# A gated-linear-attention and mixture-of-experts layer on eight cores: each sequence divided 18 tiles and 14 instead of 16 and 16, with the code of the two halves chosen by a flag

## The chip, the cores and the metric

The kernel runs on all 8 cores of one Trainium2 chip, four sequences of 4096 tokens, two cores for each sequence. The cores exchange nothing. The metric is device time in microseconds (us) of the slowest core. Before the change it is 1550.89 us, the median of 3 runs (1548.65 to 1551.49).

## The reference

Each token is a row of 1024 numbers. With `xn = layernorm(x)` the layer returns `x + attention(xn) + ffn(xn)`. Cut to what matters:

```
q, k, v = xn@Wq, xn@Wk, xn@Wv            # 4 heads: 256, 256 and 512 wide
g  = logsigmoid(xn@Wgk1@Wgk2 + b) / 16   # a decay for each channel of the key
S_t = exp(g_t) * S_{t-1} + k_t^T v_t     # state 256 x 512 for each head, along the sequence
o_t = q_t @ S_t * 256**-0.5
attention = (rmsnorm(o) * rms_w * silu(xn@Wg)) @ Wo
ffn = xn + sum over the 2 best of 4 experts of w_e * LN(relu(LN(xn@W1_e+b1))@W2_e+b2)
```

The state S runs through the whole sequence, so the core with the later tokens needs the state that the earlier tokens leave.

## The kernel before

**Work and stages.** A tile is 128 tokens. Every core owns 16 tiles (`T = 2048`), in four blocks of four, and runs one and the same program.

1. *Prefix* (`p_LN`, `p_T`, `p_gk`, `p_scan`, `p_Eop`, `p_K`, `p_KT`, `p_M`): the state that the first 2048 tokens of the sequence leave. For each block of four tiles the rows are normalized (ScalarE, `p_xtm`), transposed on TensorE (`p_xT`), the decays go through exp and ln on ScalarE and a running sum on VectorE (`p_L`), and the keys are multiplied by them (`p_kd`) and transposed by DMA (`p_kdT`). `p_M` sums x^T k over all 16 tiles (256 matmuls), and 64 more matmuls with Wv give the state `s_W`. All eight cores do this; on the cores with the first half the result is multiplied by 0 (L718, `cvals[:, 3]`).
2. *Attention*: four blocks. A block has 16 groups of silu gates (`groupG`, 8 matmuls each), and then four units, one for each head (`unit`): queries and keys (`groupQ`, `groupK`), values (`groupV`), the next head's decays (`gates`), and woven between them (`merge`) the recurrence of the unit before (`gla_A`, `gla_C`, four steps). `gla_end` scales the four output rows-blocks of a unit by their rms (L963, VectorE), transposes them by DMA and stores them to the DRAM tensor `og_d`. The next block's tokens are loaded, normalized and transposed as side work of units 0 and 1, the router (`m_route`) in unit 2. In the last block unit 1 carries `lists`, which sorts the tokens by expert: 32 indirect DMAs write the lists to DRAM, one after another on GpSimd (L1129).
3. *Output projection* (`wo_head`, `wo_half`): for each tile 34 matmuls, with `s_ogl` loaded back from `og_d` (`load_ogl`, 2 MB a block) and the token rows `s_xr`. In the same stretch GpSimd issues the expert weights (`load_e`): float32 in DRAM, cast to bfloat16 by the DMA on its way to SBUF, 16 pieces an expert.
4. *Experts*: 35 slots (`NSLOT`) of 128 token rows each. A slot's rows are gathered by indirect DMA, transposed by DMA (`s_xgT`), and go through `f_z1` (16 matmuls, VectorE adds b1 and takes statistics), a norm (`s_zh`), `f_th` (8 transposes on TensorE, 8 relus on ScalarE), `f_z2` (16 matmuls, VectorE adds b2 and takes statistics), a norm (`s_z`), a multiplication (`s_y`) and an indirect DMA that adds the rows to the output. The stages of neighbouring slots are interleaved in one hand-written loop.

**What sets the order.** Every engine runs its own list in program order, and a helper `P.emit` puts the semaphore waits in front. SyncE's queue carries all transposing DMAs, the `s_ogl` loads and the stores of the output; GpSimd's queue carries the weights, the loads of x in the attention stage, the stores to `xn_d` and `og_d`, the list writes, and gathers; ScalarE's queue the `s_xr` loads. Within a queue a DMA whose wait isn't over holds all behind it. The addresses of an expert's weights come from registers that TensorE and VectorE load at each slot (L89), and six slots have one conditional wait on TensorE (`wait_if`).

Line 334 is every plain matmul (`mm`), 339 every transpose on TensorE, 343 every plain DMA of GpSimd, 348 and 350 SyncE's; so the rows are told apart by their tiles.

## Time and profile before

| | |
|---|---|
| Median of 3 runs | 1550.89 us |
| The profiled execution | 1549.63 us, with a span of 1548.1 us from the first to the last instruction of its slowest core (core 1) |
| Spans of the 8 cores | 1542.5, 1548.1, 1509.7, 1528.1, 1511.6, 1513.7, 1515.4, 1513.2 us |
| Busy, core 1 | TensorE 1088.4 us (70%), VectorE 679.7 (44%), ScalarE 570.8 (37%), GpSimd 213.4 (14%) |
| Chain that ended last | TensorE 43%, issue 15%, VectorE 14%, ScalarE 11%, DMA 9% |

On core 1 the prefix lasts to 327 us, the attention blocks to 926, the output projection to 1151, and the experts to the end. PE is TensorE, PEld its weight loads, DVE VectorE, ACT ScalarE, POOL GpSimd, SP SyncE; "q" behind one of these is its instruction queue. The time behind `<-` in square brackets is what ended the idle time ahead of an instruction, inferred from semaphores.

### The profile page before, as it was taken

The page shows a single profiled execution, that of the slowest core. Times are in us where ns is not written, and L with a number is a line of the kernel's source. Part 1 is how long each engine was busy: PE and PEld are TensorE (multiplying, and loading weights), DVE is VectorE, ACT ScalarE, POOL GpSimd, SP SyncE. Part 2 cuts the span into 40 slices and gives each one's busy share as a digit, 9 for nine tenths or more (in the row PEclk, how much of TensorE's full clock was granted, in tenths as well). Part 3 has the DMA queues.
Part 4 walks back from the last instruction along what each step waited for, and adds up shares of the span by engine and source line. Part 5 has one row for each costly group of instructions (what it writes and reads, how often), then busy time and mean ns, then how long its engine had stood idle before and what let it go on. Part 6 is the DMA issues. An engine that isn't in the chain of part 4 may idle for free.

```text
span 1548.1 us, 21016 instructions; the slowest of 8 cores (1509.7 to 1548.1 us)
## 1 busy us (share of the span) xinstructions
PE 1088.4 (70%) x4906; PEld 461.4 (30%) x4906; DVE 679.7 (44%) x1340; ACT 570.8 (37%) x1095; POOL 213.4 (14%) x266
## 2 busy tenths in 40 slices
PE   2347484998798589858888453966487777777772
PEld 1123131433333233323333121422133333333331
DVE  2353342012573266326635443410015666776664
ACT  3633411043434334434444111210104656565653
POOL 3000010000000000000001532050012222222211
PEclk9977586877999799979999766987688999999996
DMA  9931058501221422144119127999739756556643
GB/s 202 157 82 28 0 82 163 82 28 38 60 67 28 116 49 55 28 116 69 35 28 151 22 50 198 221 224 196 214 84 158 133 104 109 95 104 108 105 73 57
DMA packets 171934, 151.66 MB, mean 98 GB/s; under 512 B 127500, under 2 KB 139820, under 8 KB 171792
## 3 DMA queue, kind: packets, MB, share of 16 engines
q0 software_dynamic: 41168, 86.61, 30.4%
q1 hardware_dynamic: 128352, 55.33, 17.4%
q10 hardware_dynamic: 2304, 8.39, 1.7%
q8 instruction: 53, 0.87, 0.3%
q14 instruction: 57, 0.47, 0.1%
HBM read 117.84 MB, written 40.21 MB: 102 GB/s over the span
## 4 chain that ended last, share of the span: by engine, by line
PE 43%; issue 15%; DVE 14%; ACT 11%; DMA 9%; another core or an unknown queue 2%; DVEq 2%; SPq 2%; ACTq 0%; POOL 0%; POOLq 0%
PE pb L334 39%; DMA s_ogl<-og_d 4%; PE pb L1319 3%; ACT s_hT L1387 2%; DVE s_bnf L1334 2%; DVE p_L L509 2%; ACT s_zh L1372 2%; SPq L348 1%; PE pb L339 1%; DVE s_L L822 1%; DVE s_bn L407 1%; DMA s_xgT<-s_xg 1%; DVE s_bn L408 1%; DVE s_z L1324 1%
## 5 line engine op out<-in xcount | busy, mean ns | idle before, releaser
L334 PE MATMUL pb<-s_wo,s_ogl 128*128 128x512 bf16 x512 | 123.4, 397 | 77.4 <-DMA s_ogl<-og_d 77.1
L1319 PE MATMUL pb<-s_we,s_xgT 128*128 x560 | 132.4, 392 | 29.3 <-DMA s_xgT<-s_xg 13.5
L334 PE MATMUL pb<-s_wv,s_xnT 128*128 128x512 bf16 x512 | 131.1, 405 | 14.2 <-ACT s_v L890 6.3
L334 PE MATMUL pb<-s_wg,s_xnT 128*128 128x512 bf16 x512 | 129.0, 415 | 14.4 <-ACT s_silu L841 13.9
L938 DVE SCALAR_TENSOR_TENSOR s_W<-s_W,s_eb,pb 128x512 bf16<-128x512 bf16 x128 | 89.8, 742 | 96.1 <-PE pb L334 62.3
L1319 PE MATMUL pb<-s_we,s_hT 128*128 x560 | 128.6, 384 | 0.0
L1387 ACT ACTIVATE s_hT<-pb,s_gbs 128x128 bf16<-128x128 bf16 x280 | 103.9, 450 | 10.7 <-PE pb L339 9.7
L1324 DVE TENSOR_TENSOR s_z<-pb,s_b 128x512 bf16<-128x512 f32 x140 | 90.4, 685 | 27.4 <-PE pb L1319 21.1
L1185 DVE TENSOR_TENSOR s_xr<-s_xr,pb 128x512 f32<-128x512 f32 x32 | 22.0, 688 | 172.3 <-PE pb L334 172.3
L944 ACT ACTIVATE s_sq<-pb 128x512 bf16<-128x512 f32 x64 | 38.2, 596 | 158.9 <-PE pb L334 109.8
L1418 POOL DMA_INDIRECT out<-s_y,s_list x35 | 55.2, 1577 | 276.1 <-DVE s_z L1324 264.1
L334 PEld LDWEIGHTS pb<-s_wo,s_ogl 128*128 128x128 bf16 x512 | 49.4, 101 | 140.8 <-issue 90.9
L1319 PEld LDWEIGHTS pb<-s_we,s_xgT 128*128 128x128 bf16 x560 | 55.9, 100 | 105.0 <-issue 51.5
L334 PE MATMUL pb<-p_kdT,p_xtm 128*128 128x512 bf16 x256 | 68.1, 437 | 23.1 <-DMA p_kdT<-p_kd 23.1
L334 PE MATMUL pb<-s_xnT,s_wk 128*128 128x512 bf16 x256 | 66.7, 413 | 23.1 <-DVE s_qg L856 19.8
L1339 ACT ACTIVATE s_rf<-s_mvf,c_cv 128x1 f32<-128x1 f32 x70 | 20.7, 295 | 158.4 <-DVE s_mvf L1335 157.4
L334 PEld LDWEIGHTS pb<-s_wg,s_xnT 128*128 128x128 bf16 x512 | 53.1, 105 | 86.3 <-issue 46.7
L334 PEld LDWEIGHTS pb<-s_wv,s_xnT 128*128 128x128 bf16 x512 | 49.9, 102 | 88.5 <-issue 43.1
L334 PE MATMUL pb<-s_W,s_qg 128*128 128x512 bf16 x128 | 42.2, 392 | 42.9 <-issue 29.0
L339 PE MATMUL pb<-c_id,p_xtm 128*128 128x128 bf16 x128 | 15.5, 308 | 80.8 <-ACT p_xT L469 44.2
L1319 PEld LDWEIGHTS pb<-s_we,s_hT 128*128 128x128 bf16 x560 | 54.2, 99 | 59.5 <-issue 3.2
L339 PE MATMUL pb<-c_id,s_zh 128*128 128x128 bf16 x280 | 21.6, 221 | 70.0 <-ACT s_zh L1372 70.0
(192 smaller groups left out, 1597.8 us busy)
## 6 DMA issues: line engine op xcount, KB each, us to landing
s_we<-W POOLq DMA_DIRECT2D x64, 256.0 KB, 26.0
p_x<-xp_tm SPq DMA_DIRECT2D x16, 512.0 KB, 8.1
og_d<-s_ogT POOLq DMA_DIRECT2D x16, 512.0 KB, 3.6
s_xr<-x_tm ACTq DMA_DIRECT2D x16, 512.0 KB, 8.4
s_ogl<-og_d SPq DMA_DIRECT2D x16, 512.0 KB, 15.6
out<-s_xr SPq DMA_DIRECT2D x16, 512.0 KB, 8.4
s_x<-x_tm POOLq DMA_DIRECT2D x12, 512.0 KB, 6.3
s_wv<-Wv POOLq DMA_DIRECT2D x4, 1024.0 KB, 48.8
```

The source lines that it names most:

```text
L334: lambda e: e.matmul(out=out, lhsT=lhsT, rhs=rhs, start=start, stop=stop),
L339: lambda e: e.transpose(out=out, in_=in_, identity=c_id[:, :]),
L509: t = V(lambda e, kc=kc: e.tensor_tensor_scan(out=p_L[:, par, kc, :], data0=c_one5[:, :].broadcast_to([128, 512]), data1=p_L[:, par, kc, : ...
L938: W_tok[kc] = V(lambda e, pi=pi, kc=kc: e.scalar_tensor_tensor(out=s_W[:, kc, :], in0=s_W[:, kc, :], scalar=s_eb[:, kc, 4 * b + c:4 * b + ...
L944: ka = A(lambda e: e.activation(out=s_sq[:, :], in_=bk[oi], func=ACT.Square, accum_out=s_ssq[:, par, 0, c:c + 1]), wait=[to] + sq_tok[0] + ...
L1185: k = V(lambda e: e.tensor_tensor(out=xs, in0=xs, in1=bk[bi], op=ALU.add), wait=[t, tb_tok[n]])
L1319: t = P.emit("tensor", lambda e, dc=dc: e.matmul(out=bk[bi], lhsT=lhs[:, dc, :], rhs=P.window("tensor", e, ("w", s, hf), s_we[layer][dc], ...
L1324: k = V(lambda e: e.tensor_tensor(out=zt[:, hf * 512:(hf + 1) * 512], in0=bk[bi], in1=P.window("vector", e, ("v", s), bvec, 512, hf * 512) ...
L1334: t = V(lambda e: e.bn_stats(out=bn[:, 6:12], in_=zt[:, 512:1024]), wait=[k1])
L1372: return lambda: A(lambda e: e.activation(out=s_zh[p][:, :], in_=s_z1[p][:, :], func=ACT.Identity, scale=s_rf[:, p, 0:1], bias=s_rf[:, p, ...
L1387: k = A(lambda e, dc=dc: e.activation(out=s_hT[p][:, dc, :], in_=bkh[bi][:, dc * 128:(dc + 1) * 128], func=ACT.Relu, scale=s_gbs[:, p, dc: ...
L1418: S[s]["put"] = P.emit("gpsimd", lambda e: e.indirect_dma_start(out=out_d, out_offset=bass.IndirectOffsetOnAxis(ap=s_list[:, s, 0:1], axis=0),
```

## The change

1. **The split.** The first core of a pair owns 18 tiles in blocks of 4, 2, 4, 4, 4 and the second 14, in blocks of 2, 4, 4, 4. A flag in DRAM, loaded into a register of each engine, picks between two bodies (`Prog.branch`): the first core runs `first_block` (no prefix; block 0, and the gates of block 1), the second `earlier` (prefix over 18 tiles, and the gates of block 1). Then all engines wait until TensorE, VectorE and ScalarE have reached that point (`P.meet`), and both run the same code. Three more branches: the loads of block 0's `s_ogl`, its four tiles of output projection, and the last slots. The first core has 39 expert slots, the second 31 (`NS1`).
2. **The prefix written finer.** `earlier` weaves the pieces of one block's keys (`p_K`, by chunk) with the transposes, decays and statistics of the next blocks.
3. **Queues.** On the first cores Wg is loaded ahead of Wk. x for a block is loaded at the start of the block before's gates instead of in its first unit; x and `xn_d` of the first tiles go by SyncE. `load_ogl` for the first block needed stands inside the last attention block, and the later ones three and four tiles ahead of their use. The list writes are issued one by one from `scatter`, each behind a TensorE count.
4. **Rows scaled one unit later.** `gla_end` only computes the rms; the scaling, the transposing DMA and the store move to `gla_out`, called from `flush` in the middle of the next unit.
5. **Expert weights.** `cast_e`, 32 pieces of 1 MB float32, DRAM to DRAM with a cast to bfloat16, one or three a unit from block 1 on. `load_e` then loads bfloat16 from ScalarE's queue, four pieces a tile of the output projection.
6. **Expert slots.** b2 is added by one more matmul with a single row (`z2_half`), the second layer's statistics and norm read PSUM directly (`f_stats2`, `f_norm2`), and `f_norm2` stands behind `f_z1` and `f_th`. b2 is loaded as one partition.

The diff, cut:

```diff
 NKC = 8
-T = 2048
-NT = T // 128
-NB = T // 512
+
+
+BASE = (0, 4, 6, 10, 14)
+TILES = (4, 2, 4, 4, 4)
+
+PBASE = (0, 2, 6, 10, 14)
+PTILES = (2, 4, 4, 4, 4)
+NT = 18
+T = NT * 128
+NB = len(BASE)
 GN = 16.0
 LN16 = float(np.log(1.0 / GN))
 EPS = 1e-5
 KB = 1024
-NSLOT = 2 * T // 128 + NE - 1
+NSLOT = 2 * NT + NE - 1
+NS1 = 2 * (NT - BASE[1]) + NE - 1
 
 
...
+    def branch(self, body1, body0):
+
+
+        begin = {s: s.n for s in self.owner}
+        at = {eng: len(self.q[eng]) for eng in self.ENGINES}
+        ways = []
+        for body in (body1, body0):
+            for s in self.owner:
+                s.n = begin.get(s, 0)
+            body()
+            part = {}
+            for eng in self.ENGINES:
+                part[eng] = self.q[eng][at[eng]:]
+                del self.q[eng][at[eng]:]
+            ways.append((part, {s: s.n for s in self.owner}))
+        end = {s: max(w[1].get(s, begin.get(s, 0)) for w in ways) for s in self.owner}
+        for s, n in end.items():
+            s.n = n
...
+            def run(e, eng=eng, fill=fill):
+                with e.If(self.vals[eng]["flag"] > 0):
+                    one(e, ways[1][0][eng], fill[1])
+                with e.Else():
+                    one(e, ways[0][0][eng], fill[0])
+            if ways[0][0][eng] or ways[1][0][eng] or fill[0] or fill[1]:
+                self.q[eng].append(run)
+
+    def meet(self, toks):
+
+        for eng in self.ENGINES:
+            def run(e, toks=tuple(toks)):
+                for s, v in toks:
+                    e.wait_ge(s.h, v)
+            self.q[eng].append(run)
...
+    P.branch(lambda: None, wg_first)
     for hf in range(2):
         k_wk = gdma(s_wk[:, :, hf * 512:(hf + 1) * 512], rows(Wk[:, hf * 512:(hf + 1) * 512]),
                     d_wk)
...
+    def earlier():
+        for h in range(H - 1):
+            load_wv(h)
+        for n in range(4, 8):
+            load_xp(n)
+        for i in range(4):
+            p_T(4, i)
...
+        for b in (4, 3, 2, 1, 0):
+            n = b - 1
+            for kc in range(NKC):
+                p_K(b, kc)
+                if b >= 2 and kc < PTILES[b - 2]:
+                    p_st(PBASE[b - 2] + kc)
+                if b >= 1:
...
+        ev2 = p_M(2, [0, 1, 2, 3], every, True, True, ev0)
+        ev3 = p_M(3, [4, 5, 6, 7], every, True, True, ev1)
+        load_wv(H - 1, [(te, te.n)])
+
+        V(lambda e: e.memset(s_eb[:, :, BASE[1]:BASE[1] + 1], 1.0))
+        for a in (s_sel, s_is0, s_w, s_wb):
+            V(lambda e, a=a: e.memset(a[:, 0:BASE[1], :], 0.0))
+        s_ev = []
+        rot.banks, rot.mark = [4, 5, 6], [list(ev3) for _ in range(3)]
+        for kc in range(NKC):
+            bi = kc % 4
+            if kc == 3:
+                m_gk1(1)
+            elif kc == 5:
+                gates(H)
+            elif kc == 7:
+                m_route(1)
+            w = [k_wv[kc // 2]]
```

`load_wg` is called in `wg_first` on the first cores; `load_ogl`, `wo_head` and `wo_half` are as before, with tile numbers.

```diff
+    def flush():
+
+        while late:
+            gla_out(late.pop(0))
 
...
+        t = A(lambda e: e.activation(out=s_ssq[:, par, 1, 0:nt], in_=s_ssq[:, par, 1, 0:nt],
                                      func=ACT.Exp, scale=-0.5), wait=[t])
-        kv = (ve, ve.n)
-        for c in range(4):
+        rs_tok[u] = [t, (ve, ve.n)]
+
+    def gla_out(u):
+
+        par = u % 2
+        nt = TILES[u // 4]
+        for c in range(nt):
             k = V(lambda e, c=c: e.tensor_scalar(
                 out=s_og[par][:, c, :], in0=s_og[par][:, c, :],
                 scalar1=s_ssq[:, par, 1, c:c + 1], scalar2=None, op0=ALU.mult),
...
+    scatters = []
+
+    def scatter():
+
+        if not scatters:
+            return
+        tc, k, w = scatters.pop(0)
+        P.emit("gpsimd", lambda e: e.indirect_dma_start(
+            out=list_d,
+            out_offset=bass.IndirectOffsetOnAxis(ap=r_row[:, k, tc:tc + 1], axis=0),
+            in_=r_pair[:, k, tc, :], in_offset=None), wait=w + [(te, te.n)], inc=d_sc, inck=16)
+        if not scatters:
+            k_list.append(gdma(s_list[:, :, :].rearrange("p s k -> p (s k)"),
+                               list_d.rearrange("(p s) k -> p (s k)", p=128), d_li,
+                               wait=[(d_sc, d_sc.n)]))
 
...
+    def cast_e(i):
+
+        n = D // 4
+        e, l, q = i // 8, i // 4 % 2, i % 4
+        cast.append(i)
+        gdma(wb_d[i * n:(i + 1) * n, :], (W1, W2)[l][e, q * n:(q + 1) * n, :], d_wb[e])
 
...
     def load_e(e, wait, part=range(16)):
-        o = e_off[e] // 2
...
-                          wait=wait if i == 0 else [])
+            row = (2 * e + l) * D + dc * 128
+            P.emit("scalar", lambda x, l=l, dc=dc, row=row: x.dma_start(
+                out=s_we[l][dc].ap[:, e_off[e] // 2:e_off[e] // 2 + D],
+                in_=wb_d[row:row + 128, :]),
+                wait=(list(wait) + [(d_wb[e], 8 * 16)]) if i == part[0] else [], inc=d_e[e],
+                inck=16)
```

```diff
+    def block_G(b, steps):
+
+        if b + 1 < NB:
+            m_load(BASE[b + 1])
+            m_load(BASE[b + 1] + 1)
+        gg = [lambda h=h, i=i: groupG(b, h, i) for h in range(H) for i in range(TILES[b])]
+        n = max(len(gg) * 11 // 16, min(len(gg), len(steps)))
+        merge(gg[:2], [])
+        flush()
+        merge(gg[2:n], steps)
+        merge(gg[n:], [])
...
+            for _ in range(0 if b == 0 else 1 if b in (1, NB - 1) else 3):
+                cast_e(len(cast))
...
+    P.branch(earlier, first_block)
+    P.meet([(te, te.n), (ve, ve.n), (sc, sc.n)])
+    block_units(1)
+    for b in range(2, NB):
+        block_G(b, gla_list(4 * b - 1))
+        gla_end(4 * b - 1)
+        late.append(4 * b - 1)
+        block_units(b)
+    u = NB * H - 1
...
+    def wo_run(lo, hi):
+        for q in range(lo, hi):
+            if q == 3:
+                load_ogl(3)
+            if q == 6:
+                load_ogl(4)
+                load_vec(0, s_b1, b1b, att_done + [wo_te[(2, 3)], ogl_tok[3]])
+            if q == 10:
+                P.branch(lambda: None, lambda: load_ogl(0))
+            wo_head(q)
+            if q + 1 < NT:
+                wo_load(q + 1)
+
+            if q < 7:
+                load_e(0, [proj_te[NB - 1]], range(4 * q - 12, 4 * q - 8))
+            elif q < 11:
+                load_e(1, att_done, range(4 * q - 28, 4 * q - 24))
+            elif q < 14:
+                load_e(2, att_done, range((16 * (q - 11) + 2) // 3, (16 * (q - 10) + 2) // 3))
+            for hf in range(2):
+                wo_half(q, hf)
+                scatter()
...
+    for s in range(4):
+        f_gather(s)
+    for s in range(4):
+        f_xpose(s)
+    P.branch(lambda: None, lambda: wo_run(NT - BASE[1], NT))
+    wo_done = [(te, te.n), (ve, ve.n), (sc, sc.n)] + [(q, q.n) for q in d_ob + d_xr]
...
+    def z2_half(s, hf, lw):
+
+        bi, w = rotZ.next()
+        t = z_mm(s, 1, hf, s_hT[s % 2], (bi, w + lw), False)
+        t = P.emit("tensor", lambda e: e.matmul(
+            out=bk[bi], lhsT=c_ones[0:1, :],
+            rhs=P.window("tensor", e, ("v", s), s_b2, 512, hf * 512), start=False, stop=True),
+            wait=[k_vec[1], k_c1], inc=te)
+        S[s][f"z2{hf}"] = (bi, t, rotZ.i % len(rotZ.banks))
+        return t
+
...
+    def f_stats2(s):
+        (b0, t0, _), (b1, t1, _) = S[s]["z20"], S[s]["z21"]
+        S[s]["ta2"] = z_stats(bk[b0], bk[b1], 2 + s % 2, t0, t1)
+        S[s]["r2"] = z_rstd(2 + s % 2, S[s]["ta2"])
 
...
@@ -1452,13 +1834,34 @@
             relu(range(4, NDC))
         if own:
             S[s]["zh"] = norm1()
-        if 2 <= s < NSLOT + 2:
+        if 2 <= s < n + 2:
             f_z2(s - 2)
+            f_stats2(s - 2)
```

**Where instructions move: VectorE in an expert slot.** Before, from the multiplication `s_y` to the next slot's register loads. `s_z_132` is the second layer's row (b2 is `s_b_115`), `s_rf` the scale and shift of a norm, `s_list` the router's weight.

```order
L1414 TENSOR_TENSOR s_y_117<-s_z_133,s_g_113 128x1024
L1347 SCALAR_TENSOR_TENSOR s_rf<-s_mvf,s_rf 128x1
L1324 REGISTER_ALU
L1324 TENSOR_TENSOR s_z_132<-pb,s_b_115 128x512
L1324 REGISTER_ALU
L1324 TENSOR_TENSOR s_z_132<-pb,s_b_115 128x512
L1333 BN_STATS s_bnf<-s_z_132 128x6
L1334 BN_STATS s_bnf<-s_z_132 128x6
L1335 BN_AGGR s_mvf<-s_bnf 128x2
L1346 TENSOR_TENSOR s_rf<-s_rf,s_list 128x1
L1347 SCALAR_TENSOR_TENSOR s_rf<-s_mvf,s_rf 128x1
L89 TENSOR_LOAD r_sl x2
```

Now, the same stretch of a slot (here `s_b_115` is b1 and `s_z_128` the first layer's row):

```order
L1690 TENSOR_TENSOR s_z_128<-pb,s_b_115 128x512
L1723 TENSOR_TENSOR s_rf<-s_rf,s_list 128x1
L1724 SCALAR_TENSOR_TENSOR s_rf<-s_mvf,s_rf 128x1
L1710 BN_STATS s_bnf<-s_z_128 128x6
L1711 BN_STATS s_bnf<-s_z_128 128x6
L1712 BN_AGGR s_mvf<-s_bnf 128x2
L1795 REGISTER_ALU
L1795 TENSOR_TENSOR s_y_117<-s_z_133,s_g_114 128x1024
L1724 SCALAR_TENSOR_TENSOR s_rf<-s_mvf,s_rf 128x1
L1710 BN_STATS s_bnf<-pb 128x6
L1711 BN_STATS s_bnf<-pb 128x6
L1712 BN_AGGR s_mvf<-s_bnf 128x2
L151 TENSOR_LOAD r_sl x2
```

The two additions of b2 are gone and the second layer's statistics read PSUM; the two small operations on the older slot's scale (with `s_list`) stand ahead of the first layer's statistics, and the register loads follow the second layer's aggregation directly.

**SyncE, around the end of the last attention block.** `s_kdT` are transposed keys, `s_ogT` transposed outputs, `s_ogl` the loads for the output projection. Before:

```order
L348 DMA_TRANSPOSE s_kdT_73<-s_kd_71 128x8x128
L348 DMA_TRANSPOSE s_ogT_84<-s_og_66 128x8x128 x2
L348 DMA_TRANSPOSE s_kdT_72<-s_kd_70 128x8x128
L348 DMA_TRANSPOSE s_ogT_85<-s_og_67 128x8x128 x2
L348 DMA_TRANSPOSE s_kdT_73<-s_kd_71 128x8x128
L348 DMA_TRANSPOSE s_ogT_84<-s_og_66 128x8x128 x2
L350 DMA s_ogl_88<-og_d 128x2048 x4
L350 DMA s_ogl_89<-og_d 128x2048 x4
L350 DMA out<-s_xr_90 128x1024
L350 DMA out<-s_xr_91 128x1024
L350 DMA out<-s_xr_92 128x1024
```

Now:

```order
L468 DMA_TRANSPOSE s_kdT_73<-s_kd_71 128x8x128
L468 DMA_TRANSPOSE s_kdT_72<-s_kd_70 128x8x128
L468 DMA_TRANSPOSE s_ogT_85<-s_og_66 128x8x128 x2
L470 DMA s_ogl_89<-og_d 128x1024 x4
L468 DMA_TRANSPOSE s_kdT_73<-s_kd_71 128x8x128
L468 DMA_TRANSPOSE s_ogT_86<-s_og_67 128x8x128 x2
L468 DMA_TRANSPOSE s_ogT_85<-s_og_66 128x8x128 x2
L470 DMA s_ogl_90<-og_d 128x2048 x4
L470 DMA out<-s_xr_91 128x1024
L470 DMA out<-s_xr_92 128x1024
L470 DMA out<-s_xr_93 128x1024
```

The first load of `s_ogl` moved ahead of the last unit's keys, and the second block's stands ahead of the first store as before, now behind only one pair of transposes.

**GpSimd, in the last attention block.** `s_wo` is Wo, `list_d` the list writes, `s_we` the expert weights, `wb_d` their bfloat16 copy. Before:

```order
L343 DMA s_wo<-Wo 128x4x1024 x4
L343 DMA s_be_94<-be2r 4x1024
L1129 DMA list_d<-r_pair,r_row 8192x2 x32
L343 DMA s_list<-list_d 128x128
L343 DMA og_d<-s_ogT_84 128x2048
L343 DMA og_d<-s_ogT_85 128x2048
L343 DMA og_d<-s_ogT_84 128x2048
L343 DMA s_we_0_97<-W 128x1024
L343 DMA s_we_1_98<-W 128x1024
```

Now:

```order
L463 DMA s_wo<-Wo 128x4x1024 x4
L463 DMA s_be_95<-be2r 4x1024
L463 DMA wb_d<-W 16x16384
L463 DMA og_d<-s_ogT_86 128x2048
L463 DMA wb_d<-W 16x16384 x2
L1344 DMA list_d<-r_pair,r_row 8192x2 x4
L463 DMA og_d<-s_ogT_85 128x2048
L1344 DMA list_d<-r_pair,r_row 8192x2 x4
L463 DMA wb_d<-W 16x16384
L1344 DMA list_d<-r_pair,r_row 8192x2 x4
L463 DMA og_d<-s_ogT_86 128x2048
L1344 DMA list_d<-r_pair,r_row 8192x2 x4
```

The 32 list writes were one run ahead of three stores of outputs; 36 now stand in groups among the stores, and the weights' loads have left this queue for casts placed earlier.

## Rows read from the trace of the kernel before

**Rows 1.** Each core's span (us) and mean granted TensorE clock (1.0 is full speed)

```profile
core 1: 1548.1 us, clock 0.870
...
core 4: 1511.6 us, clock 0.851
```

**Rows 2.** Where TensorE waited on core 1: us in total, times, longest

```profile
PE pb L334 <- DMA s_ogl<-og_d: 77.1, 3, 27.8
PE pb L339 <- ACT s_zh L1372: 70.0, 32, 6.0
...
PE pb L334 <- issue: 30.4, 7, 29.0
PE pb L334 <- DVE s_kd L870: 28.8, 5, 13.1
...
PE pb L334 <- DMA p_kdT<-p_kd: 23.1, 1, 23.1
```

**Rows 3.** Core 1 by stretch: length; busy PE, PEld, DVE, ACT, POOL; clock; DMA share; GB/s

```profile
0.00:40.00 40.00, 11.80 (x48) 4.88 (x48) 11.46 (x29) 15.71 (x23) 15.36 (x28) 1.00 1.00 200
...
253.80:327.00 73.20, 73.20 (x272) 29.88 (x272) 10.14 (x23) 15.66 (x25) 5.07 (x8) 0.79 0.40 73
331.90:367.80 35.90, 35.04 (x130) 14.14 (x130) 4.70 (x19) 13.55 (x22) 0.00 (x0) 0.78 0.07 20
367.80:464.60 96.80, 81.39 (x380) 33.66 (x378) 57.51 (x109) 39.55 (x76) 4.36 (x8) 0.93 0.28 66
464.60:616.00 151.40, 120.77 (x551) 50.56 (x551) 73.01 (x135) 59.10 (x112) 6.45 (x12) 0.90 0.27 63
130.00:184.00 54.00, 30.83 (x129) 13.23 (x128) 23.60 (x39) 22.43 (x33) 0.00 (x0) 0.69 0.11 20
766.00:926.00 160.00, 108.31 (x472) 45.47 (x471) 66.19 (x135) 47.73 (x89) 38.17 (x42) 0.84 0.34 57
926.00:1151.00 225.00, 147.08 (x625) 59.04 (x623) 49.13 (x95) 27.52 (x38) 33.65 (x61) 0.82 0.82 191
...
1250.00:1500.00 250.00, 187.63 (x977) 85.49 (x974) 170.84 (x365) 150.04 (x342) 60.79 (x47) 1.00 0.59 102
```

**Rows 4.** Timeline of TensorE in core 1's start (start, us, instruction, idle time before)

```profile
38.98 1.16 PE L334 MATMUL pb<-p_gk,s_wgk 16*128 16x512 bf16 x2 [2.09 <-ACT p_L L494]
...
77.31 12.87 PE L334 MATMUL pb<-p_xT,s_wk 128*128 128x512 bf16 x51
```

**Rows 5.** All engines of core 1 in the second attention block

```profile
524.32 0.69 DVE L407 BATCH_NORM_STATS2 s_bn<-s_x 128x6 f32<-128x512 f32 x1 [11.29 <-DMA s_x<-x_tm]
...
528.19 0.58 PE L334 MATMUL pb<-s_gk,s_wgk 16*128 16x512 bf16 x1 [13.10 <-DVE s_kd L870]
```

**Rows 6.** TensorE of core 4 at its start of the output projection

```profile
923.21 1.01 PE L334 MATMUL pb<-s_wo,s_ogl 128*128 128x512 bf16 x2 [28.20 <-DMA s_ogl<-og_d]
```

**Rows 7.** TensorE of core 1 in one expert slot and the next slot's start

```profile
1259.54 0.61 PE L339 MATMUL pb<-c_id,s_zh 128*128 128x128 bf16 x8 [1.92 <-ACT s_zh L1372]
...
1264.06 3.61 PE L1319 MATMUL pb<-s_we,s_xgT 128*128 x16 [0.46 <-issue]
1269.68 0.49 PE L339 MATMUL pb<-c_id,s_zh 128*128 128x128 bf16 x6 [2.00 <-ACT s_zh L1372]
```

**Rows 8.** VectorE of core 1 in the same slot

```profile
1267.64 1.28 DVE L1324 TENSOR_TENSOR s_z<-pb,s_b 128x512 bf16<-128x512 f32 x2
...
1273.36 0.17 DVE L1312 COPY s_gbs<-s_gb 128x16 f32 x1 [1.65 <-ACT s_z L1408]
```

**Rows 9.** The page's queues: packets, MB, share of 16 engines' span

```profile
q0 software_dynamic: 41168, 86.61, 30.4%
...
q10 hardware_dynamic: 2304, 8.39, 1.7%
```

**Rows 10.** DMA issues: KB each, us to landing; the whole run, then 1151 to 1200 us

```profile
s_xgT<-s_xg SPq DMA_TRANSPOSE x35, 3.1
...
s_xgT<-s_xg SPq DMA_TRANSPOSE x7, 10.1
```

1149 lines of the change are left out of this document (664 added, 485 removed).

## The prediction

> **What bounds the kernel now.** I read the spans of the cores first. Core 1 is the slowest and core 4 stands for the other die, 36 us earlier [rows 1]. Both clocks are near 0.86 of full speed, so the difference has to be sought in waits. Next come TensorE's waits by releaser [rows 2]; five of them matter: 77.1 us at three block starts of the output projection, 70.0 us in 32 slots for the norm `s_zh`, one stretch of 29.0 us in which nothing shown was waited for, 28.8 us behind the keys `s_kd`, and 23.1 us at the prefix's last transpose. Then the stretches [rows 3]: in attention TensorE is busy for 80% of a block (120.77 of 151.4 us), in the output projection for 65%, in the experts for 75%. So TensorE's own list bounds the kernel, with holes that others cut into it, and any work that a core is spared counts nearly in full. The prefix and its start take the first 327 us of all cores, and on the four first cores its result is multiplied by 0.
>
> Every matmul has 512 columns or fewer, and the engine runs at either level: 16 matmuls take 3.61 us in a slot at a granted clock of 1.00 [rows 7], 0.226 us each, which is the 2.4 GHz level; over the prefix's `p_M` the 272 matmuls take 73.20 us, 0.269 each, at 0.79 [rows 3].
>
> **The change part by part, first cores.** The prefix goes, 16 tiles become 18. All times count from the span's start.
>
> *Start.* The silu gates of block 0 need x (2.1 MB), Wg (8.4 MB as float32), and for the decays' scan also Wk (4.2) and the constants (1.3), 16 MB in all. The first 40 us move 200 GB/s with the DMA engines wholly busy [rows 3], so 80 us. Low bound 45 (the gates start once x and the first half of Wg are there and the scan is hidden under them), high 85. I take 80, as the gates of 35.9 us are then still ahead of the units.
>
> *Blocks.* Block 0 is as before, 35.9 + 96.8 = 132.7 us [rows 3]: to 212. A block in the steady state takes 151.4 us [rows 3]. From it goes the 13.1 us wait for which VectorE stood 11.29 us at x [rows 5], since x is now issued a whole gate stage earlier, and I take 4 us for VectorE's four row scalings and the transposes that no longer stand ahead of the first unit's keys (28.8 us over five waits, 13.1 of them the one above, leave 15.7 for four [rows 2]); casts may cost 5. 151.4 - 13.1 - 4 + 5 = 139, taken as 138. The 2-tile block is half of that, 69, plus 6 for the meeting of the engines and for the operations whose count doesn't halve: 75, to 287. Two blocks of four, 276: to 563. The last block took 160.0, with the 29.0 us hole in it [rows 2, 3]. In the hole all engines but GpSimd stand, while its 32 list writes run; they are now spread over the following stage, so 160 - 29 - 4 = 127, to 690. If the hole isn't the list writes, it stays: the high bound of this term is +29.
>
> The Trainium skill has a rule that speaks against this part (Runtime: NRT & Kernel Launch, Instruction fetch mechanics): prefetch is sequential, and a taken branch to code outside of the current window stalls the engine on a fetch. No row shows what such a stall costs here; the nearest is the 29.0 us hole, and the `issue` wait at a slot's start is 0.46 us [rows 7]. With the one, five branches would cost 145 us if each fell on the path, with the other 2 us; the sum holds 6 us for the meeting alone.
>
> *Output projection.* 225 us with 77.1 us of waits for `s_ogl` [rows 2, 3]. Core 4 shows the same wait of 28.20 us at its stage start [rows 6], so it is no accident of core 1. There SyncE's first load stands behind the last unit's transposes and the stores on GpSimd behind the list writes. Both go: the first load is issued in the last block, the others three and four tiles ahead. 225 - 77 = 148 for 16 tiles; a tile more costs 34 matmuls at 147.08 / 625 = 0.235 us, 8.0 us, so 148 + 16 = 164. I leave 8 us of waits: 172, to 862. Bounds: 164 and 241 (no wait goes).
>
> *Slots.* Before, a slot takes 10.14 us, from one row `s_zh` x8 at 1259.54 to the next at 1269.68 [rows 7]. TensorE is busy 187.63 us in 250 [rows 3], 7.6 in a slot, and the two idle pieces are 2.00 + 0.46. The 2.00 is VectorE's chain: adding b1, statistics, norm. In its list stood two additions of b2 of 1.28 us together and the wait of 1.65 us for `s_z` [rows 8]; the additions go, statistics read PSUM, and the second layer's norm stands behind the first's. TensorE gets two matmuls of one row more, at most 0.45 us. 7.6 + 0.45 = 8.05 is the floor; with the 0.46 and nothing else 8.5; with only 1.28 less and 0.45 more 9.3. Register loads on both engines stay, and statistics from PSUM may cost more than the 0.68 us from SBUF. I take 9.6, nearer to the old value than the chain allows, since 1.65 us of waits for ScalarE are not touched. Bounds 8.6 and 10.4. 39 x 9.6 = 374. The stage had 397 us for 35 slots: 397 - 355 = 42 for the way in and out; the first gathers are now issued four tiles early, 36. 862 + 374 + 36 = 1272.
>
> **Second cores.** *Prefix, 18 tiles.* The block in 130 to 184 us takes 54.0 us with TensorE busy for 30.83, DVE 23.60, ACT 22.43 [rows 3]. No engine is full: the transposes and decays of the next block stood between key groups instead of within them. Woven, the floor is 31, and I take 38. First keys came at 77.31, and the first block's decays ended at 38.98 + 1.16 [rows 4]; between them stood the second block's rows, now woven in. So the start is between 41 and 77, taken as 56. 56 + 4.5 x 38 = 227. The rest of `p_M` is 224 matmuls at 0.269 us: 60, to 287; the 23.1 us hole at the last transpose [rows 2] goes because a part of the sum for the four older blocks stands behind it. `s_W`: 17 plus 5 for its pieces, to 309; small ones and the gates of the 2-tile block (half of 35.9, less what is woven): 20, to 329. Its units and the meeting 61: to 390. 276 + 127 as above: 793. Output projection of 14 tiles: 148 - 16 + 8 = 140, to 933. 31 x 9.6 + 42 = 340: 1273.
>
> So both halves end together by this sum, with 1 us between them. That the sum balances is not needed for the gain, the later one counts. The slowest of eight cores was 36 us behind the other die's [rows 1], 29 of it the hole that I took away; I add 10 us for a core that has some of that again. 1273 + 10 = 1283, and 1.5 us lie outside the span (1549.6 against 1548.1): 1285. The profiled execution is 1.3 us under the median of the runs, which I leave.
>
> **What hides the rest.** The casts: 32 pieces, 50 MB of traffic, move from the output projection (191 GB/s, DMA 0.82 [rows 3]) to blocks at 63 GB/s and 0.27. Three pieces in a unit of 35 us are 4.7 MB more, 136 GB/s, together 199: just what the start sustains. If the rings don't share well, loads of x and stores of outputs behind them on GpSimd come late. The transposes are the most exposed: 3.1 us over the run, 10.1 us where the weights stream in [rows 10], that is 7 us once in each unit. The keys' transpose has a unit's recurrence ahead of it, which covers it; without the cover 15 units x 7 us = 105 us.
>
> The Trainium skill (DMA: Bandwidth & Descriptors, Queues, rings and completion order) says that a DMA engine goes round between the rings packet by packet, so a small transfer waits for others' packets but never for a whole piece. By that the 10.1 us are about the worst, and the trace agrees so far.
>
> **Rivals.**
> *A, the output projection becomes DMA-bound and the slots don't move.* On the second cores, 33 MB (weights in bfloat16, `s_ogl`, token rows in and out) want to pass in about 120 us, 280 GB/s; mixed traffic reached 191 here, and 8.39 MB in 1.7% of the engines' span is 319 GB/s for plain loads, 86.61 MB in 30.4% is 184 for the casting ones [rows 9]. At 191 GB/s the stage is 173 us, 33 later; with the first cores at 241 it is 69 later. Slots at 10.15 add 0.55 x 39 = 21. Together 1285 + 69 + 21 = 1375 at most. For it: DMA share 0.82. Against: half of the bytes are gone.
> *B, the prefix doesn't compress*: 54 us a block, 4.5 x 16 = 72 more on second cores alone: 1357. Against: three engines under 60%. For: ScalarE's chain of exp and ln is serial.
> *C, better*: starts at 50 us, slots at 8.6: 1285 - 30 - 39 = 1216. For: the floor of 8.5.
> *D, slower*: a DRAM to DRAM piece with 16 rows of 64 KB holds the GpSimd ring. x and the output rows stand in that queue in turn with 12 pieces a block. The two blocks of 24 pieces take 276 us; to lose 266 us (1551 - 1285) they'd have to be 542, 22.6 us a piece, 46 GB/s. A piece at 200 GB/s is 5.2 us, so this needs a quarter of the 184 GB/s that casting loads reach [rows 9]. At 25 us a piece the time is 1285 + 24 x 25 - 276 = 1609.
> *E, the halves don't come apart*: if the code of both bodies cost its time on every core, the 212 us of block 0 would stand ahead of the second cores' way: 1285 + 212 = 1497. Against: an engine's register picks one body, and the other holds no wait.
>
> **Chances.** Forecast 0.69, own range 1235 to 1335 (the bounds of start, slots and one hole, not all on one side); A 0.13, B 0.08, C 0.06, D 0.03, E 0.01. Range for 8 in 10: 1222 to 1370. A difference under 0.2% can't be told from none here. Faster 0.96, within 0.2% 0.01, slower 0.03.
>
> **What would show it.** The first gates on first cores at 60 to 80 us and the end of attention near 690; keys every 38 us in the prefix on second cores; no wait for `s_ogl` over 8 us; no hole of 29 us with GpSimd alone busy; slot rows `s_zh` 9.6 us apart, VectorE's statistics from PSUM under 0.8 us; a cast piece landing in 5 to 15 us. Wrong would be: a wait for x or `og_d` in blocks 2 and 3 over 10 us (D), one half of the cores ending over 40 us ahead of the other, or slots at 10.1 with the wait now at a register load.

## The result, and the profile after

| | before | after |
|---|---|---|
| Median | 1551.49 us (5 runs, 1548.65 to 1586.75) | 1211.06 us (5 runs, 1205.46 to 1250.12) |
| Ratio | | 0.7798, 95% interval 0.7763 to 0.7833 |
| Profiled execution | 1549.63 us | 1205.46 us, span 1203.7 us (core 0) |

The kernel became 340 us faster. The prediction said 1285 us, 266 us faster, with a range down to 1222: the direction is right, the size is not, and the time lies below the range. Medians are over all runs of a kernel; in some runs the cores of one die show a lower clock and end later (1586.75 and 1250.12 here), and the ratios and the ranges in brackets further down leave these out, so that a ratio and two medians can differ by up to a per cent.

The spans of four cores, in answer to [rows 1]. The first cores of the pairs are the even ones, the second the odd ones.

```profile
core 0: 1203.7 us, clock 0.941
core 1: 1190.8 us, clock 0.930
...
core 4: 1200.4 us, clock 0.941
core 5: 1189.0 us, clock 0.939
```

All first cores end within 4 us of one another, all second ones within 3, and the two kinds are 12 us apart. The granted clock rose from 0.85 to 0.88 on the eight cores to 0.93 and 0.94. There is no straggling die any more.

TensorE's waits on core 0, in answer to [rows 2] (us in total, times, longest):

```profile
PE pb L454 <- ACT s_silu L1010: 36.8, 1, 36.8
PE pb L454 <- DVE s_W L1116: 20.0, 27, 2.0
...
PE pb L459 <- ACT s_zh L1748: 6.6, 4, 2.9
PE pb L454 <- DVE s_kd L1041: 6.0, 5, 2.3
...
PE pb L454 <- DMA s_ogl<-og_d: 5.2, 1, 5.2
...
PE pb L454 <- issue: 1.6, 6, 0.4
```

The 77.1 us for `s_ogl` are 5.2 (9.9 in one wait on core 1), the 70.0 for `s_zh` are 6.6, the 28.8 for `s_kd` 6.0, the hole of 29 us is gone. One wait is new as a single piece: 36.8 us at the very start, while VectorE waits for the constants that stand behind Wg and Wk in GpSimd's queue.

Stretches of core 0, in answer to [rows 3] (length; busy us and count on PE, PEld, DVE, ACT, POOL; granted clock; DMA share; GB/s). The start with block 0's gates, block 0's units, the 2-tile block, the three 4-tile blocks, the output projection and 250 us of experts:

```profile
0.00:101.00 101.00, 41.68 (x174) 17.96 (x175) 15.28 (x29) 25.66 (x38) 21.12 (x35) 0.81 1.05 180
101.00:194.50 93.50, 80.02 (x405) 34.70 (x404) 56.35 (x116) 38.94 (x77) 1.09 (x2) 0.96 0.28 57
194.50:285.80 91.30, 67.96 (x376) 34.41 (x375) 49.49 (x111) 40.18 (x82) 5.86 (x11) 0.91 0.55 96
285.80:413.90 128.10, 113.38 (x531) 48.37 (x532) 67.48 (x125) 57.78 (x111) 14.15 (x27) 0.96 0.61 119
413.90:542.70 128.80, 114.56 (x545) 49.26 (x544) 72.64 (x134) 58.18 (x112) 11.41 (x22) 0.96 0.64 123
542.70:673.00 130.30, 111.81 (x506) 48.09 (x504) 77.71 (x161) 48.10 (x96) 22.86 (x28) 0.93 0.55 99
673.00:837.00 164.00, 151.41 (x656) 61.28 (x656) 39.39 (x75) 26.63 (x29) 33.36 (x40) 0.96 0.93 278
900.00:1150.00 250.00, 242.75 (x1232) 107.13 (x1229) 176.21 (x381) 179.23 (x436) 73.94 (x58) 0.99 0.71 124
```

And of core 1: one block of the prefix, the last matmuls of `p_M`, from `s_W` to the end of the 2-tile block, a 4-tile block and the projection of 14 tiles:

```profile
82.00:115.00 33.00, 21.93 (x111) 9.28 (x110) 21.98 (x40) 21.73 (x31) 0.00 (x0) 0.84 0.28 64
190.90:245.00 54.10, 51.84 (x242) 23.38 (x241) 4.30 (x8) 3.50 (x7) 1.75 (x2) 1.00 0.81 142
245.00:338.60 93.60, 74.91 (x439) 38.09 (x438) 40.80 (x113) 42.85 (x84) 7.84 (x14) 0.95 0.44 93
469.30:598.50 129.20, 114.44 (x546) 49.23 (x545) 72.64 (x134) 58.36 (x112) 11.41 (x22) 0.97 0.62 120
729.50:871.00 141.50, 123.05 (x517) 49.24 (x517) 33.17 (x63) 20.40 (x24) 24.19 (x28) 0.91 0.93 260
```

A slot of the experts is now TensorE's: 242.75 us busy in 250, against 187.63 before. TensorE's and VectorE's rows of one slot, in answer to [rows 7, 8]:

```profile
1058.90 0.61 PE L459 MATMUL pb<-c_id,s_zh 128*128 128x128 bf16 x8
1059.34 1.89 PE L1679 MATMUL pb<-s_we,s_hT 128*128 x8
1061.17 0.39 PE L1701 MATMUL pb<-s_b,c_ones 1*128 x1
1061.48 1.90 PE L1679 MATMUL pb<-s_we,s_hT 128*128 x8
1063.32 0.39 PE L1701 MATMUL pb<-s_b,c_ones 1*128 x1
1063.79 3.61 PE L1679 MATMUL pb<-s_we,s_xgT 128*128 x16
1067.24 0.61 PE L459 MATMUL pb<-c_id,s_zh 128*128 128x128 bf16 x8
```

```profile
1056.28 0.70 DVE L1710 BATCH_NORM_STATS2 s_bnf<-pb 128x6 f32<-128x512 f32 x1
...
1058.82 0.18 DVE L1672 COPY s_gbs<-s_gb 128x16 f32 x1 [0.93 <-ACT s_rf L1716]
```

From `s_zh` to `s_zh` it is 1067.24 - 1058.90 = 8.34 us, and over 31 slots of this core 8.56 on average. TensorE follows without a gap that is marked, and the shortest slots of the core are 8.20 us. The statistics from PSUM take 0.70 us where those from SBUF took 0.68, so reading PSUM cost at most 0.02 us more here.

Where the first cores' time went, stage by stage, against the sum of the prediction:

| stage, first cores | forecast | measured | off |
|---|---|---|---|
| start and block 0 | 212 | 194.5 | -17.5 |
| 2-tile block | 75 | 91.3 | +16 |
| two 4-tile blocks | 276 | 128.1 + 128.8 | -19 |
| last block | 127 | 130.3 | +3 |
| projection, 18 tiles | 172 | 164 | -8 |
| 39 slots, lead-in and tail | 410 | 366.7 | -43 |
| slowest of eight | 10 | 0 | -10 |
| sum | 1282 | 1203.7 | -78 |

### The profile page after: what moved, and what is told of

Read it like the earlier page. It is cut to its first block, busy times and chain, and to the rows that moved or that the text cites. A ratio compares the mean times of both kernels' runs of the same rounds, so it can differ in the third digit from the quotient of the medians.

```text
span 1203.7 us, 21686 instructions; the slowest of 8 cores (1189.0 to 1203.7 us)
## 1 busy us (share of the span) xinstructions
PE 1008.6 (84%) x4822; PEld 437.4 (36%) x4822; DVE 614.5 (51%) x1259; ACT 538.1 (45%) x1128; POOL 205.2 (17%) x239
## 4 chain that ended last, share of the span: by engine, by line
PE 56%; ACT 12%; issue 10%; DMA 10%; DVE 8%; POOL 1%; DVEq 1%; SPq 1%; ACTq 0%; POOLq 0%
PE pb L454 39%; PE pb L1679 15%; DMA out<-zpad 4%; ACT s_hT L1763 3%; DMA s_xr<-x_tm 2%; DMA out<-s_xr 2%; DVE s_L L991 2%; ACT s_z L1787 1%; PE pb L459 1%; ACT s_sq L1122 1%; DMA out<-s_y,s_list 1%; ACT s_Em L997 1%; PE pb L1701 1%; ACT s_v L1066 1%; ACT s_L L988 1%
## 5 line engine op out<-in xcount | busy, mean ns | idle before, releaser
L454 PE MATMUL pb<-s_wv,s_xnT 128*128 128x512 bf16 x576 | 151.0, 412 | 25.7 <-ACT s_v L1066 11.9
L454 PE MATMUL pb<-s_wg,s_xnT 128*128 128x512 bf16 x576 | 133.1, 390 | 37.2 <-ACT s_silu L1010 36.8
L1679 PE MATMUL pb<-s_we,s_xgT 128*128 x624 | 144.8, 386 | 11.8 <-ACT s_hT L1763 3.9
L1679 PE MATMUL pb<-s_we,s_hT 128*128 x624 | 149.2, 382 | 0.0
L1763 ACT ACTIVATE s_hT<-pb,s_gbs 128x128 bf16<-128x128 bf16 x312 | 116.4, 459 | 5.2 <-PE pb L459 3.4
L1787 ACT ACTIVATE s_z<-pb,s_rf 128x512 bf16<-128x512 f32 x78 | 56.4, 773 | 76.9 <-DVE s_rf L1724 74.3
L991 DVE TENSOR_TENSOR_SCAN s_L<-c_rst,s_L 128x512 f32<-128x512 bf16 (+1 forms) x40 | 42.5, 1104 | 76.2 <-DMA out<-zpad 38.8
L1679 PEld LDWEIGHTS pb<-s_we,s_hT 128*128 128x128 bf16 x624 | 56.5, 98 | 65.2 <-issue 10.6
L454 PE MATMUL pb<-s_xnT,s_wk 128*128 128x512 bf16 (+1 forms) x320 | 68.4, 366 | 11.2 <-DVE s_qg L1026 11.0
L1010 ACT ACTIVATE s_silu<-pb 128x512 bf16<-128x512 f32 x72 | 42.3, 597 | 77.8 <-PE pb L454 76.3
L454 PE MATMUL pb<-s_xnT,s_wq 128*128 128x512 bf16 (+1 forms) x320 | 67.9, 366 | 7.5 <-DVEq L107 5.1
L1400 ACT ACTIVATE s_xr<-s_xr,s_rs 128x1024 f32<-128x1024 f32 x18 | 22.3, 1238 | 108.5 <-DMA s_xr<-x_tm 108.5
L454 PE MATMUL pb<-s_W,s_qg 128*128 128x512 bf16 x144 | 47.5, 389 | 20.8 <-DVE s_W L1116 20.0
```

Source lines behind the costliest of these rows:

```text
L454: lambda e: e.matmul(out=out, lhsT=lhsT, rhs=rhs, start=start, stop=stop),
L991: ts = V(lambda e, k=k: e.tensor_tensor_scan(out=s_L[:, k, 0:N], data0=c_rst[:, 0:N], data1=s_L[:, k, 0:N], initial=0.0, op0=ALU.mult, op1 ...
L1010: k = A(lambda e: e.activation(out=s_silu[:, i, h * HDV:(h + 1) * HDV], in_=bk[bi], func=ACT.Silu), wait=[t] + ([silu_free[(h, i)]] if (h, ...
L1400: tb_tok[q] = A(lambda e: e.activation(out=s_xr[q % 4][:, :], in_=s_xr[q % 4][:, :], func=ACT.Identity, scale=s_rs[:, 2, n:n + 1], bias=s_ ...
L1679: t = P.emit("tensor", lambda e, dc=dc: e.matmul(out=ps, lhsT=lhs[:, dc, :], rhs=P.window("tensor", e, ("w", s, hf), s_we[layer][dc], 512) ...
L1763: k = A(lambda e, dc=dc: e.activation(out=s_hT[p][:, dc, :], in_=bkh[bi][:, dc * 128:(dc + 1) * 128], func=ACT.Relu, scale=s_gbs[:, s % 3, ...
```

## The experiments

The kernel before took 1533 us on one chip and 1551 on another (medians), so each group of runs has its own value of it. The changed kernel itself was run in two groups: 1211.1 us in that of the result and 1207.6 in that of ctl, x_scale, split_only and best. A price taken from another group is a difference between chips and good to some us only; for these, read the stages and slots of the trace first. In s_vadd, s_old and split_only b1's rows stand in for b2's, so these three don't compute the layer, and only their times are read. "Changed kernel" is the one of the diff; all edits are on it unless said otherwise.

### The expert slot: which of its edits shortened it

**s_vadd.** Additions of the second layer's bias on VectorE again, statistics and norm from SBUF, no bias matmul.

```diff
-        t = z_mm(s, 1, hf, s_hT[s % 2], (bi, w + lw), False)
-        t = P.emit("tensor", lambda e: e.matmul(out=bk[bi], lhsT=c_ones[0:1, :], rhs=b2 ...
+        t = z_mm(s, 1, hf, s_hT[s % 2], (bi, w + lw), True)
+        k = V(lambda e: e.tensor_tensor(out=s_z2[...], in0=bk[bi], in1=<s_b1>, op=ALU.add), ...
```

> The changed kernel, but the second layer's bias is added by VectorE (two additions of 1.28 us a slot, b1's rows standing in for b2's) and its statistics and norm read SBUF; the extra matmuls are gone; the order of the slot stays new. Theory A, the additions made the old slot long: slots 9.5 us instead of 8.3, 39 x 1.2 = 47 us, about 1255 us. Theory B, the place of the second layer's norm made it long: TensorE loses two matmuls and VectorE stays inside its slack, slots 8.0 to 8.4, 1200 to 1212 us.

Measured: 1282.3 us (1276.0 to 1284.2 in four of five runs). TensorE waits 55.1 us for `s_zh` in the 250 us where it waited hardly at all, and slots are 10.7 us. Theory A, and more than it asked for.

**s_n2first.** `f_norm2(s - 3)` moved back ahead of `f_z1(s)`.

> The changed kernel with only the second layer's norm put back ahead of the next slot's first layer; statistics from PSUM and the bias matmul stay. Theory A (the additions): nothing, 1205 to 1213 us. Theory B (the order): TensorE waits 1.9 us a slot for the norm of the first layer again, slots 9.8 to 10.1 us, 1265 to 1280 us. Both together needed: 1225 to 1240 us.

Measured: 1228.9 us (1223.7 to 1228.9), ratio 0.7924 with an interval of 0.7814 to 0.8033: some 17 us over the changed kernel, slots 9.0 us. By the ratios this isn't clear of noise; by the slots it is (8.96 against 8.55 us between 900 and 1150 us on core 0). Neither theory's number: with the additions gone the order counts, for about a quarter of the whole.

**s_old.** Both.

> The changed kernel with both put back: additions on VectorE (b1's rows standing in for b2's) and the norm of the second layer ahead. Both theories: the old slot of 10.1 us, 39 x 1.8 = 70 us, 1278 us. If it stays under 1250 us, something else in the change shortened the slots too.

Measured: 1266.5 us (1264.1 to 1269.2), slots 10.2 us, as before the change [rows 7]. With the additions there, the old order is even better than the new one, by 16 us (s_vadd against s_old, one group).

**b_n2late.** The kernel before, with `f_norm2(s - 3)` moved behind `f_z1(s)` and `f_th(s - 1)`.

> The kernel before with one thing moved: the second layer's norm stands behind the next slot's first layer and transposes. Theory A (the additions): 1551 us, no change. Theory B (the order): slots 8.6 us instead of 10.14, 35 x 1.5 = 53 us less, about 1498 us.

Measured: 1556.7 us median, its least 1539.7, against 1546.5 for the kernel before (least 1541.5) in the same group. No gain can be seen, and the median slot is 10.6 us on every core where it was 10.1. Two neighbours, among the shorter ones:

```profile
1359.74 0.69 PE L339 MATMUL pb<-c_id,s_zh 128*128 128x128 bf16 x8 [3.12 <-ACT s_zh L1372]
...
1369.80 0.61 PE L339 MATMUL pb<-c_id,s_zh 128*128 128x128 bf16 x8 [0.87 <-ACT s_zh L1372]
```

The wait for `s_zh` is in place. So the order alone makes the old slot 0.5 us longer, as s_vadd against s_old says too; it is worth something only once the additions are gone. What was open is whether the additions cost by VectorE's time or by the way through SBUF.

**dummy2** and **dummy1.** The changed kernel with two, or one, additions that write where the norm writes later:

```diff
+        for hf, (bi, t) in enumerate(((b0, t0), (b1, t1))):     # dummy1: b0 alone
+            V(lambda e, bi=bi, hf=hf: e.tensor_tensor(out=s_z2[...half hf], in0=bk[bi],
+                in1=<s_b1>, op=ALU.add), wait=[t] + ...)
         S[s]["ta2"] = z_stats(bk[b0], bk[b1], 2 + s % 2, t0, t1)
```

> The changed kernel with two additions more on VectorE in each slot, of the form and at the place of the old additions of b2; their result is overwritten unread, and statistics and norm still read PSUM, the bias matmul stays. If VectorE's time in its chain sets the slot: 10.1 to 10.4 us a slot, 1275 to 1290 us, as with the real additions. If the way through SBUF did it: VectorE is 6.2 us busy in a slot of 8.3, has room for 1.3, and the time stays under 1215 us.

> The same with one addition (0.65 us) a slot. If each added us of VectorE counts in full from the first on: slots 8.95 us, 25 us more than the changed kernel, 1235 us. If there is slack first and a jump behind it: under 1220 us. If any delay of the statistics costs a whole round: 1270 us.

Measured: 1290.0 us with two (ratio 0.8368, 0.8333 to 0.8402) and 1239.0 with one (0.8024, 0.7999 to 0.8049). Slots are 10.9 and 9.4 us. TensorE's waits in 900 to 1150 us with two, and two neighbouring slots:

```profile
PE pb L1679 <- ACT s_z L1792: 28.7, 22, 1.7
PE pb L459 <- ACT s_zh L1748: 25.2, 22, 1.3
```

```profile
1053.45 0.61 PE L459 MATMUL pb<-c_id,s_zh 128*128 128x128 bf16 x8 [1.16 <-ACT s_zh L1748]
...
1064.32 0.61 PE L459 MATMUL pb<-c_id,s_zh 128*128 128x128 bf16 x8 [1.15 <-ACT s_zh L1748]
```

Nobody reads what the two wrote, and the way through SBUF is not taken. VectorE's time in its chain is thus enough to explain the slot. The first 0.65 us cost 0.8 us a slot, the second 1.5. With two, neither engine is full: of 10.9 us TensorE is busy for 8.4 and VectorE for 7.2. So the slot isn't a sum but a ring of waits between three engines: VectorE's statistics, ScalarE's norm that frees the PSUM bank (the wait for `s_z` above), and TensorE.

### The attention blocks

**x_late.** The loads of x moved from the start of the gates into the first unit.

```diff
-        if b + 1 < NB:
-            m_load(BASE[b + 1])
-            m_load(BASE[b + 1] + 1)
```

> The changed kernel, x of the next block loaded in the first unit again instead of at the start of the gates. Theory A, the waits of a block went one by one with their causes: a wait of about 13 us for x in each of three blocks comes back on every core, about 1240 to 1250 us. Theory B, VectorE's scalings were the cause and x would have come in time: 1205 to 1215 us.

Measured: 1216.3 us (1211.2 to 1217.0), 1533.0 before in this group. The two middle blocks of core 0 take 126.5 and 129.2 us (126.3 and 129.2 in ctl), no wait of 13 us. Theory A is wrong.

**scale_now.** `gla_out` called directly after `gla_end`.

```diff
             gla_end(u - 1)
-            late.append(u - 1)
+            gla_out(u - 1)
```

> The changed kernel, rows scaled, transposed and stored directly after the rms again, not one unit later. Theory A: about 4 us a block, 5 blocks, 1225 to 1230 us. Theory B (the scalings made the waits): 10 us or more a block, over 1250 us. Rival C: nothing, the scalings had found idle time on VectorE (busy 0.56 of a block), 1205 to 1213 us.

Measured: 1243.5 us (1236.1 to 1245.0). On core 0 the two middle blocks take 132.6 and 135.2 us, the last 133.2, and the projection 177 instead of 164. It is worth 32 us by the medians (two chips), twice the four times 4 us that I gave it.

**x_scale.** Both.

> The changed kernel with x loaded in the first unit and rows scaled and stored at once, both as before. With x late alone the blocks kept their 128 us; with the scaling alone they took 133 to 135. Theory C: the old 13 us wait came from GpSimd's queue, where the x loads stood behind the store of the last unit's outputs, which waits for their transposes; each of the two edits alone takes that away. Then both back give blocks of 145 to 150 us, 3 x 15 = 45 us over the changed kernel plus the 13 to 19 us that the scaling alone costs later: about 1275 us. Theory D (two separate costs, 0 and 6 us a block): 133 to 136 us a block, 1240 to 1245 us.

Measured: 1271.7 us (1254.5 to 1272.7), against 1207.6 for the changed kernel in the same group (**ctl**, below). Blocks of 141 and 146 us on core 0 and 149 and 150 on core 1. GpSimd's queue in the first unit of a 4-tile block of core 0, and TensorE behind it:

```profile
473.43 0.54 POOL L463 DMA_DIRECT2D og_d<-s_ogT  x1 [33.63 <-DMA s_ogT<-s_og]
473.96 1.07 POOL L463 DMA_DIRECT2D s_x<-x_tm  x2
```

```profile
289.20:430.70 141.50, 113.81 (x521) 48.04 (x531) 67.53 (x125) 58.30 (x112) 12.46 (x24) 0.93 0.52 105
```

```profile
482.84 0.58 PE L454 MATMUL pb<-s_gk,s_wgk 16*128 16x512 bf16 x1 [12.29 <-DVE s_kd L1041]
```

The loads of x were ready to go but stand behind a store that waits 33.63 us for its transposes, and TensorE loses 12.29 us, the 13.10 of [rows 5]. They leave 43 us after the block's start. With x late alone they leave 9 us after it (421.4, the block from 412.3), with the scaling alone also 9 us (428.6, from 419.6). Theory C: one cause of the 13 us wait, two remedies, each sufficient for it; the scaling's other 4 to 7 us a block come on top.

**ctl.** The changed kernel itself.

> The changed kernel again, unaltered, on the chip of the next three: the kernel before took 1533 us on one chip and 1551 on another, so times of two chips are not to be compared. 1205 to 1213 us if this chip is like the first, ratio 0.776 to 0.783.

Measured: 1207.6 us (1200.1 to 1213.4), 1548.2 before in this group.

### The projection and its queues

**w_f32.** No `cast_e`; `load_e` as before from float32, on GpSimd's queue.

```diff
-                cast_e(len(cast))
-            P.emit("scalar", lambda x, ...: x.dma_start(out=s_we..., in_=wb_d[row:row + 128, :]) ...
+            gdma(s_we..., (W1, W2)[l][e, dc * 128:(dc + 1) * 128, :], d_e[e], ...)
```

> The changed kernel without casts in DRAM: the expert weights are loaded as float32 and cast on the way by GpSimd's queue during the output projection, as before. Theory A, the projection would be bound by DMA traffic: it takes 164 us now with the DMA engines 0.93 busy at 278 GB/s; 17 MB more to read and the casting rate of 184 to 200 GB/s give 225 us and a start of the experts that waits, 1265 us or more. Theory B, the loads of s_ogl alone made the 77 us of waits: under 1225 us. In the attention blocks, which lose the casts, A and B both expect 128 us a block, as now.

Measured: 1239.5 us (1236.9 to 1240.1). The projection did not become longer, as theory A has it, but shorter: 149 us for 18 tiles (668.9 to 818.1), TensorE busy for 147 of them, at 244 GB/s and a DMA share of 0.96. Then the experts' first matmul waits for rows, not for weights by its row; on core 1 the wait is 49.83 us:

```profile
853.08 3.15 PE L1674 MATMUL pb<-s_we,s_xgT 128*128 x7 [34.63 <-DMA s_xgT<-s_xg]
```

`s_xgT` are the gathered rows, transposed. Their gathers are issued at 798 to 802 us, behind 32 weight loads in GpSimd's queue (779 to 797 us), and take up to 51 us to land. That the weights hold them up is read from this order; no run separates it. Blocks without casts: 126.3, 129.1 and 129.9 us, and with casts, in ctl, 126.3, 129.2 and 129.9. So the casts cost the blocks nothing that can be seen, and the total is 28 us longer rather than 54, by another way than theory A's.

**list_run.** The 36 list writes in one run.

```diff
+        while scatters:
+            scatter()
         yield
```

> The changed kernel, the 36 list writes issued in one run as soon as the lists are ready, as before. Theory A (the run of writes on GpSimd caused the 29 us hole): a hole of 25 to 30 us in the last block on some or all cores, or GpSimd's stores of outputs late and a wait for s_ogl of the same length: 1225 to 1240 us. Theory B (the hole was core 1's own, from another cause): 1205 to 1213 us.

Measured: 1249.8 us. In the profiled execution the first cores end at 1219 and 1220 us on one die and at 1239 and 1241 on the other, and this is the hole: in the last block TensorE of cores 0 to 3 has no wait over 5.4 us, that of cores 4 to 7 waits of 28, 18, 17 and 32 us. Core 4:

```profile
PE pb L454 <- DVE s_W L1116: 61.1, 28, 28.1
```

The expectation of the next run says "no hole", which holds of cores 0 to 3 alone. Again, on another chip:

> The changed kernel with the 36 list writes in one run, a second time, since the first gave one die's cores 1219 to 1220 us and the other's 1238 to 1240. There the last attention block kept its 132 us (no hole) and the projection took 180 us instead of 164. The same again: 1220 to 1230 us, the cost of the run lies in the projection. If the 29 us hole comes in the last block on some core: 1235 us or more.

**list_run_b** measured: 1233.0 us (1231.2 to 1233.4), ratio 0.7988 (0.7962 to 0.8014). The hole is back, and this was the second case of its expectation:

```profile
PE pb L454 <- DVE s_W L1116: 55.8, 27, 26.2
```

```profile
653.50 0.63 PE L454 MATMUL pb<-s_v,s_AT 128*128 128x512 bf16 x1
...
672.35 0.60 ACT L1066 ACTIVATE s_v<-pb 128x512 bf16<-128x512 f32 x1 [25.93 <-remote]
...
679.41 0.75 DVE L1116 SCALAR_TENSOR_TENSOR s_W<-s_W,s_eb,pb 128x512 bf16<-128x512 bf16 x1 [26.69 <-remote]
```

From 653 to 679 us TensorE, VectorE and ScalarE together do nothing but one copy, while GpSimd writes lists from 628 to 674 us. The DMA engines stand as well, as this stretch of the same core shows (share 0.02, 1 GB/s):

```profile
666.00:672.00 6.00, 0.00 (x0) 0.00 (x0) 0.00 (x0) 0.00 (x0) 4.47 (x6) 0.50 0.02 1
```

Cores 0 to 3 have waits of 26, 22, 17 and 29 us, cores 4 to 7 none over 5.4 in this stage, the reverse of list_run. The profile of the kernel before has 18 to 31 us on cores 0 to 3 and none over 4.2 on the others. In the changed kernel, where the writes stand among other work and start later, no core has a wait over 5.4 us in the last block. So one die of a chip has the hole, and which one differs between runs on two chips. Why stays open; no run here tells, nor whether it is the number of writes in a row that counts (core 0 of the changed kernel issues 12 in a row at 721 to 736 us, in the projection, and has no such stop).

**ogl_late.** `load_ogl(1)` behind the last unit.

> The changed kernel with the first load of s_ogl issued after the last unit's keys instead of inside the last block. Its outputs were stored half a millisecond earlier, so it is late only by the queue: a wait of 10 to 28 us for s_ogl at the start of the projection, as the 28 us of the kernel before, 1220 to 1235 us. Rival: the 28 us came from the list writes that held GpSimd's stores of the last outputs back, and the load's place is worth 5 us or less: 1205 to 1215 us.

Measured: 1216.3 us (1216.2 to 1216.9), ratio 0.7887 (0.7869 to 0.7905). The wait for `s_ogl` at the start of the projection is 16.8 us on core 0 and 21.5 on core 1, where the changed kernel has waits of 5.2 and 9.9, and the total 5 to 14 us longer (by the medians, and by the ratios 0.7887 and 0.7798). The theory's wait came, and a part of it was given back later in the stage.

### How much is the split

**split_only.** s_old, x_scale, w_f32, list_run and ogl_late together.

> The changed kernel with all but the split, the finer prefix and the order of the start's loads put back: additions of b2 on VectorE (b1's rows standing in), its norm ahead, x late, rows scaled at once, weights as float32 in the projection, list writes in one run, s_ogl loaded after the last unit. If the parts add up: 1211 + 56 (slots) + 60 (x and scaling) + 30 (weights) + 15 (list writes) + 20 (s_ogl) = about 1390 us. If they share a resource, as DMA in the projection, less: 1350 us. If the split and the new prefix alone gave most of the 340 us: under 1320 us.

Measured: 1374.9 us. In all of its runs the cores of one die were slower than of the other (profiled: 1340 and 1306 us against 1370 and 1337). The hole of the list writes is back on the longer ones alone: 15 to 23 us in one wait on cores 4 to 7, nothing over 5.2 on cores 0 to 3. The rest of the change is worth 142 us where there is no hole (core 0: 1339.9 against 1197.9 of ctl) and 167 us by the medians, hole included; the split with the new prefix and start is worth the other 173 us of the 340. The single prices (56, 64, 28, 22, 8) add up to 178, four of them across chips: nearly additive.

### A better version

**best.** Two moves, on what the trace after shows: the 36.8 us wait at the start, and the 7 to 10 us for `p_xT` in the prefix.

```diff
-                     (s_bgk[:, :], bgk2c)):
+                     (s_bgk[:, :], bgk2c), (c_rst[:, :], resetb)):
         gdma(dst, src, d_c0)
...
-                op0=ALU.mult, op1=ALU.add), wait=[t, k_c1])
+                op0=ALU.mult, op1=ALU.add), wait=[t, k_c0])
...
                 p_K(b, kc)
+                if kc == 1 and b < NB - 1:
+                    p_scan(b, 1)
+                    if b == 0:
+                        load_wg([E_tok[0][-1]])
```

(The old places of `p_scan(n, 1)` and `load_wg` are empty.)

> The changed kernel with two small moves. On first cores the constant for the running sum of the decays is loaded ahead of Wg (in the trace VectorE waits 38.8 us for it and the gates stop from 39 to 76 us): block 0 starts 15 to 30 us earlier. On second cores the second half of a block's decays goes through VectorE inside the key groups of that block, not ahead of them (TensorE waits 7 to 10 us in three blocks): 4 to 5 us in each of three blocks. Second cores end 13 us ahead of the first now, so about 1190 us if both work, 1190 as well if only the first does, 1211 if the first doesn't, since Wq and Wv are then waited for instead.

Measured: 1185.1 us (1182.6 to 1187.6) against 1207.6 for the changed kernel (1200.1 to 1213.4) in the same group, 1.9% less, and every one of its four runs is below all four of the other. Ratio to before 0.7712. TensorE at core 0's start:

```profile
41.44 24.29 PE L454 MATMUL pb<-s_wg,s_xnT 128*128 128x512 bf16 x102 [2.86 <-ACT s_silu L1010]
...
78.31 5.77 PE L454 MATMUL pb<-s_xnT,s_wq 128*128 128x512 bf16 x15 [10.98 <-DMA s_wq<-Wq]
```

The gates run through at 41 to 66 us; then 10.98 us are waited for Wq. Block 0 ends at 173.5 instead of 192.4 us (ctl). The second move did nothing: core 1 reaches its own gates at 265.2 us, in the unaltered kernel at 264.6. Now first cores end at 1179 to 1184 us and second cores at 1177 to 1186.

## Why the prediction was wrong

**The direction and most mechanisms stood.** The start waited for its loads as said: TensorE did 24 of the 128 gate matmuls at 31 to 39 us, then stood for the scan and its constants, and the rest flowed from 76 us (80 forecast). These took 25 us where the sum had 35.9 for all; that is most of the 17.5 us of the first row of the table. The 77 us for `s_ogl`, the hole and the norm's waits went. One sign was missed on second cores: a wait for `s_ogl` of 9.9 and 8.9 us on cores 1 and 3, and at the same tile 9.0 and 11.7 us that the rows of cores 5 and 7 put down to `issue`. The halves are balanced to 12 us, forecast 1. No rival came whole: A did not, the projection's DMA engines are 0.93 busy, but at 278 GB/s instead of the 191 that I took as their limit, and TensorE is busy for 151.41 of 164 us; nor D (casts that hold GpSimd's queue), pieces land in 9.3 us and blocks without them are as long; nor B, a prefix block takes 34 us against 38 in the sum; nor E, core 1's first keys come at 63 us. Of C, the better case with a chance of 0.06, the slots of 8.6 us came and the start at 50 did not.

**The step that failed is the slot's 9.6 us.** I wrote that I took it "nearer to the old value than the chain allows, since 1.65 us of waits for ScalarE are not touched". Measured are 8.56, worth 41 of the 78 us. What was wrong is that a wait was held fixed. The rows allowed less: TensorE's own 8.05 was worked out, and VectorE's busy time is 6.9 us a slot by the same row (170.84 in 250), so neither engine kept the slot at 9.6. In a ring with TensorE a shorter list of VectorE gives back waits too, and the dummies show it: 0.65 us of VectorE's time cost 0.8, 1.3 us cost 2.3. The 1.65 us wait is what the ring leaves over; at the same copy it is 0.93 us now, and it follows another operation (`s_rf`). The additions' own 1.28 x 39 = 50 us would have been a nearer guess than the 21 that 10.14 - 9.6 makes. One term of the floor was too small, which hid part of the error: each of the two bias matmuls holds the next row back by 0.31 us or more (0.31 and 0.47 in the slot shown), 0.62 together against "at most 0.45", so the floor is 8.2 and not 8.05.

**The blocks: right sum, wrong cause, and the clock left out.** From 151.4 I took 13.1 for x and 4 for the scaling and added 5 for casts. Measured is 128.4. The x wait went, but either edit does that (x_late, scale_now, x_scale); the casts cost nothing that can be seen instead of 5; and a matmul record is shorter, 0.2119 us on average (113.38 + 114.56 over 531 + 545) where it was 0.2192 [rows 3], as the granted clock went from 0.90 to 0.96. Some 550 of them make 4 us a block, and I had held the clock at what it was. The waits and the clock hang together: in x_scale, with its waits back, the block at 289 to 431 us has a clock of 0.93 and 0.2184 us a record. The same holds of `p_M`, at 0.214 us a record (51.84 / 242) and clock 1.00 where I took 0.269.

**The 2-tile block, +16 us.** I gave 6 us for what doesn't halve. TensorE is busy for 67.96 us of the 91.3, and waits 5.1 us where the engines meet and 7.9 us for VectorE's `s_qg`. The operations don't halve with the columns: 376 matmuls against 531 and 545 in the blocks of four, 111 operations of VectorE against 125 and 134, 82 of ScalarE against 111 and 112.

**The transposes** were covered as said: those of the keys land in 5.3 us (median) and 17.1 at most on core 0, and none of TensorE's waits there names them. The 10.1 us that I called "about the worst" were a median of 7, though; the longest in the same stretch of the kernel before is 17.9 us.

**Second cores** were 82 us too slow in the sum, 48 of it ahead of the blocks (gates at 261 us instead of 309, among others by blocks of 34 us instead of 38 and `p_M` at 0.214 us a record) and some 24 in the slots (8.8 us on average instead of 9.6, times 31).

**The branches.** On all four second cores TensorE has one `issue` wait of 8.9 to 10.1 us at slot 28, where the last branch takes these cores over the code of the first cores' last slots; no first core has one over 1.1 us there. TensorE of core 1:

```profile
1119.20 0.39 PE L1701 MATMUL pb<-s_b,c_ones 1*128 x1
1128.46 6.43 PE L1679 MATMUL pb<-s_we,s_xgT 128*128 x16 [8.87 <-issue]
```

The slot takes 19.95 us on core 1 (18.9 to 20.8 on the four), since VectorE is idle there too, for 4.9 us, and the 16 matmuls behind the gap take 6.43 us instead of 3.61. The Trainium skill (Runtime: NRT & Kernel Launch, Instruction fetch mechanics) says that a taken branch to code outside of the fetched window stalls the engine until it is fetched; this row agrees, with 8.87 us at one far jump, though no run here shows that it is a fetch. The other branches show no such row on TensorE of core 0 (all `issue` waits of the plain matmuls together 1.6 us, and 5.1 us for VectorE's queue where the engines meet). The last branch isn't free on the first cores either, which run straight on. Their slot there takes 10.6 to 12.3 us, 2 to 4 more than its neighbours, on core 0 by a wait for ScalarE and 16 matmuls that take 5.18 us instead of 3.61:

```profile
1074.53 5.18 PE L1679 MATMUL pb<-s_we,s_xgT 128*128 x16 [2.48 <-ACT s_hT L1763]
```

Both bodies load the registers of three slots again at this point, which may be a part of it; no run separates that from the branch. So the price is 10 to 12 us at one jump and 2 to 4 us beside it, neither the 145 us nor the 2 us of the prediction's two readings, and the larger one falls on the cores that end 12 us earlier.

## What to carry to other kernels

Where two engines hand a buffer back and forth in a loop, the busy sum of the fuller one is the floor, and the old waits must not be carried over as fixed: they shrank with the busy time here. The floor isn't the period either (with two dummies the slot is 10.9 us at 8.4 us of work), but a dummy operation on the chip measures the ring's price in one run. A wait behind a queue can have two remedies of which either does, so put edits back one by one and in pairs before either is given the gain. A hole can sit on half of the cores: look at all eight before a trace is said to be without it. When waits go, TensorE's clock comes back as well: price the busy time at the clock of the fullest stretch too.

## What was not expected of the hardware

- Plain loads and stores with few casts moved 278 GB/s over 164 us (core 0's projection, DMA share 0.93), against 191 GB/s at 0.82 with the casting loads before [rows 3] and 244 at 0.96 with them in w_f32.
- While a run of 32 or 36 indirect list writes goes out on GpSimd, 0.96 us each with 0.30 between, TensorE, VectorE and ScalarE stopped for 17 to 32 us, and the DMA engines for most of that, on the cores of one die and never on the other, in the profiles of the kernel before, list_run and list_run_b. The die is cores 0 to 3 in two of them and cores 4 to 7 in one. With the same writes spread over the following stage it did not happen.
- The kernel before had medians of 1533 to 1551 us in five groups of runs, the changed kernel 1208 and 1211 in two.
- At one far branch TensorE stood for 8.9 to 10.1 us, and the slot was 10 to 12 us longer.
